# Error rows by a PE transpose of the predictions, cell 1's h in one operation, and a reordered phase in a two-group recurrent kernel

## What is computed

```python
encoded   = tanh(xt @ We + st @ Ue + be)                       # 24 values
new_state = tanh(xt·Wx + st·Ws + bk)                           # 8 candidates of 32
mem = concat([[encoded, err]], mem[:-1])                       # 20 entries of 25
a        = relu(mem.reshape(b, -1) @ enc_w1 + enc_b1)          # 64
agent_in = relu(a @ enc_w2 + enc_b2)                           # 16
h1, c1 = lstm(agent_in, h1, c1);  h2, c2 = lstm(h1, h2, c2)    # 16 each
gate  = softmax(h2 @ gate_w + gate_b)                          # 8
theta = clamp01(mean(|mem[:, :10, -1]|) * 2.5)
gate  = gate * theta + gate_before * (1 - theta)
st    = sum_c gate[c] * new_state[c];  pred = clamp01(st[-1]);  err = pred - yt
```

## Time and profile before

| | |
|---|---|
| median of 3 runs | 5459.47 us |
| profiled execution | 5460.57 us |
| its span, first to last instruction | 5458.7 us |
| span over 512 items | 10.66 us |
| PE matmul busy | 5391.8 us (99%) |
| VectorE, ScalarE, GpSimd busy | 4479.8, 3807.2, 2421.7 us (82, 70, 44%) |
| granted TensorE clock, mean | 0.998 |

### The profile page before, as it was taken

How to read it: one execution, slowest core, us unless ns; L and a number is a source line. 1 busy time by engine, 2 the same in 40 slices (tenths; PEclk the granted TensorE clock), 3 DMA queues, 4 the chain that set the end, 5 groups by cost and what they waited for, 6 DMA issues and landing times.

```text
span 5458.7 us, 188210 instructions
## 1 busy us (share of the span) xinstructions
PE 5391.8 (99%) x67584; PEld 3426.0 (63%) x67584; DVE 4479.8 (82%) x12336; ACT 3807.2 (70%) x9729; POOL 2421.7 (44%) x4613
## 2 busy tenths in 40 slices
PE   8999999999999999999999999999999999999998
PEld 5666666666666666666666666666666666666665
DVE  7888888888888888888888888888888888888887
ACT  5777777777767777777777777777777777777775
POOL 3444444444444444444444444444444444444444
PEclk9999999999999999999999999999999999999999
DMA  2111111111111111111111111111111111111111
GB/s 69 29 29 32 29 32 29 32 29 32 29 32 29 32 29 30 31 29 32 29 32 29 32 29 32 29 32 29 30 31 29 32 29 32 29 32 29 32 29 40
DMA packets 299285, 172.38 MB, mean 32 GB/s; under 512 B 156734, under 2 KB 263882, under 8 KB 298714
## 3 DMA queue, kind: packets, MB, share of 16 engines
q1 hardware_dynamic: 293568, 159.42, 11.2%
q10 hardware_dynamic: 5146, 3.66, 0.2%
HBM read 74.65 MB, written 2.10 MB: 14 GB/s over the span
## 4 chain that ended last, share of the span: by engine, by line
PE 95%; DVE 4%; issue 1%; DMA 0%; POOL 0%; ACT 0%; DVEq 0%; ACTq 0%; POOLq 0%
PE a_ps L366 26%; PE chain L417 17%; PE cand_ps L338 9%; PE a_ps L377 9%; PE cand_ps L347 7%; PE chain L310 5%; PE chain L317 4%; PE chain L403 4%; PE chain L293 4%; PE a_ps L388 3%; PE chain L435 3%; PE cand_ps L330 3%; DVE mixed L799 1%; DVE state L817 1%; DVE added L720 1%
## 5 line engine op out<-in xcount | busy, mean ns | idle before, releaser
L366 PE MATMUL a_ps<-hist,w_hist 125*64 125x512 f16 x12288 | 1896.3, 383 | 24.1 <-DMA w_hist<-enc_table 24.1
L817 DVE TENSOR_REDUCE state<-mixed 128x64 f32<-128x512 f32 x2048 | 1353.4, 682 | 34.2 <-POOL mixed L920 0.8
L920 POOL TENSOR_TENSOR mixed<-cand,gate 128x512 f32<-128x512 f32 x1024 | 1281.1, 1272 | 48.6 <-POOL gate L908 12.5
L554 ACT ACTIVATE cand<-cand_ps 128x512 f32<-128x512 f32 x2048 | 1101.8, 593 | 91.1 <-PE cand_ps L347 90.6
L417 PE MATMUL chain<-cell_in,cell_w 128*64 128x128 f32 x16384 | 1120.7, 278 | 19.8 <-DVE cell_in L735 19.8
L886 POOL TENSOR_TENSOR one_theta<-ones,theta 128x8 f32<-128x8 f32 x512 | 103.4, 202 | 2241.0 <-DVE theta L702 2241.0
L417 PEld LDWEIGHTS chain<-cell_in,cell_w 128*64 128x64 f32 x16384 | 889.2, 136 | 271.5 <-DVE cell_in L735 211.8
L366 PEld LDWEIGHTS a_ps<-hist,w_hist 125*64 125x64 f16 x12288 | 681.4, 109 | 536.2 <-issue 141.7
L561 ACT ACTIVATE gates<-chain 128x384 f32<-128x384 f32 x1024 | 502.0, 490 | 726.3 <-PE chain L417 726.1
L735 DVE SCALAR_TENSOR_TENSOR cell_in<-gates,tanh_c 64x128 f32<-64x128 f32 x2048 | 582.5, 284 | 127.0 <-ACT tanh_c L571 113.4
L720 DVE SCALAR_TENSOR_TENSOR added<-gates 128x256 f32<-128x256 f32 x1024 | 537.1, 524 | 141.2 <-ACT gates L561 141.2
(11 more groups left out here) (76 smaller groups left out, 6823.8 us busy)
## 6 DMA issues: line engine op xcount, KB each, us to landing
x_sb<-in_x_l SPq DMA_DIRECT2D x260, 256.0 KB, 2.7
hist<-entry_parts SPq DMA_DIRECT2D x2048, 25.0 KB
w_hist<-enc_table SPq DMA_DIRECT2D x258, 128.0 KB, 2.4
y_rows<-in_y_l SPq DMA_DIRECT2D x260, 8.0 KB
ys<-in_y ACTq DMA_DIRECT2D x1, 2048.0 KB, 16.3
preds_out<-preds SPq DMA_DIRECT2D x1, 2048.0 KB, 7.5
cand<-in_encoder ACTq DMA_DIRECT2D x1, 640.0 KB, 3.8
cell_w<-in_cell ACTq DMA_DIRECT2D x2, 256.0 KB, 4.5
```

Of the source, the lines that this page charges most:

```text
L366: nc.tensor.matmul(a_ps[g][ENC * half:ENC * half + ENC, :], w_hist[0:HROWS, w_slot(u), kk, wp, :], hist[0:HROWS, xp, k, at:at + 512], star ...
L554: ins = nc.scalar.activation(cand[:, g, q // 2, :, q % 2, :, :].rearrange("p h s c -> p h (s c)"), cand_ps[q][:, :].rearrange("p (h k) -> ...
L817: V.tensor_reduce(state[:, g, hf, 2 * pair:2 * pair + 2, :], mixed[:, pair, hf, :, :, :], AX, ALU.add)\
L920: G.tensor_tensor(mixed[:, 0, :, q, :, :], cand[:, g, 0, :, q, :, :], over_s, ALU.mult)\
```

## The change

Error rows:

- `pred_now` is laid out `(h q)` instead of `(a h l)`, and VectorE computes it (`prediction(old)`) right after the mix sums.
- PE transposes it (`prediction_transpose`, two is_transpose matmuls with a stationary operand of 4 columns, moving `ident`) into partitions 0 to 3 of `cand_ps[0]`, between `history(cur, 2, 1, 3)` and `encoded_s`.
- `errors` subtracts y from those rows in PSUM, and now stands ahead of cell 1's h. `at_least_zero` and `clamped` are gone. y lies in partitions 0 to 3.
- `w_ue` has 96 columns and `w_we` 128; the products that use them go in blocks of 32 columns: three for L317, four for L310 (before: 64 and 36).

Cell 1's h: one 128-partition operation into `h_second`; the gate logits use it in two matmuls of 64 moving columns (before: four of 32). Two VectorE copies (`keep_hidden`, after `below_peak`) bring it to `cell_in[1]`.

Copy of h: GpSimd copies all of `cell_in[1]` of a group to `cell_in[0]` (`next_hidden`, after its mixes), and the waits for it move from PE's cell 0 to the two `agent_input` operations. ScalarE's two copies are gone.

Orders: ScalarE takes the third candidates' tanh after `encoder1`. On PE one history set moves from before `encoder2` to after it, and all of `history(new, 1)` now stands between `encoder2` and `candidates_bias`. VectorE's `thetas` follow cell 1's h.

```diff
-ENTRY_ROWS = (slice(0, HALF), slice(HALF, ER))
+ENTRY_ROWS = tuple(slice(S * r, S * r + S) for r in range(ZR // S))
+CHAIN_ROWS = tuple(slice(S * r, S * r + S) for r in range(P // S))
@@ PE
+            def prediction_transpose(item):
+                g, n, u = item
+                pe.wait_ge(q_pred, n)
+                pe.wait_ge(q_cand[0], n)
+                for hf in range(HF):
+                    last = nc.tensor.matmul(cand_ps[0][0:Q, P * hf:P * hf + P],
+                                            pred_now[:, g, Q * hf:Q * hf + Q], ident[:, :], is_transpose=True, start=True, stop=True,
+                                            skip_group_check=True)
+                last.then_inc(q_predps, 1)
@@ encoded_x
-                for rows in ENTRY_ROWS:
+                for rows in CHAIN_ROWS:
@@ cell_gates
-                    pe.wait_ge(q_hnext, n)
                 else:
+                    pe.wait_ge(q_hkept, n)
@@ gate_logits
-                for hf in range(HF):
-                    for rows in CELL0_OUT:
-                        last = nc.tensor.matmul(chain[g][rows, 0:TILES * C]
-                                                .rearrange("p (a h k) -> p a h k", a=2, h=HF)[:, :, hf, :],
-                                                cell_in[1][:, g, hf, rows], gate_w[:, hf, :],
-                                                start=False, stop=True, skip_group_check=True)
+                for rows in CELL0_OUT:
+                    last = nc.tensor.matmul(chain[g][rows, 0:TILES * C], h_second[:, g, rows], gate_w[:, :],
+                                            start=False, stop=True, skip_group_check=True)
@@ PE phase
                     history(cur, 2, 1, 3)
-                    history(cur, 3, 0, 1)
+                    prediction_transpose(cur)
                     encoded_s(cur)
                 if new:
                     history_waits(new, extra)
                     history(new, 0, 0, 1)
                 if cur:
-                    history(cur, 3, 1, 2)
+                    history(cur, 3, 0, 1)
                 if old:
                     logit_bias(old)
-                if new:
-                    history(new, 0, 1, 2)
-                if old:
                     gate_logits(old)
                 if cur:
-                    history(cur, 3, 2, 3)
+                    history(cur, 3, 1, 3)
                     encoder1_now(cur)
                     bias_of_cell(cur, 0)
                 if new:
-                    history(new, 0, 2, 3)
-                    history(new, 1, 0, 2)
+                    history(new, 0, 1, 3)
                 if cur:
                     encoder2(cur)
+                if new:
+                    history(new, 1)
+                if cur:
                     candidates_bias(cur)
-                if new:
-                    history(new, 1, 2, 3)
@@ ScalarE phase
-                    at_least_zero(new)
                     encoded(new)
                     entry_high(new)
                 if cur:
-                    candidates(cur, 2)
                     exponentials(cur)
                 if new:
                     encoder1(new)
                 if cur:
-                    next_hidden(cur, 0)
+                    candidates(cur, 2)
@@ VectorE
-                dve.wait_ge(q_rl, n)
-                V.scalar_tensor_tensor(entry[ZR:ER, g, :], clamped[ZR:ER, g, :], 1.0,
-                                       y_rows[ZR:ER, x_slot(u), g, :], ALU.min, ALU.subtract)\
+                dve.wait_ge(q_predps, n)
+                V.tensor_tensor(entry[ZR:ER, g, :], cand_ps[0][0:Q, 0:COLS], y_rows[0:Q, x_slot(u), g, :],
+                                ALU.subtract)\
+            def second_hidden(item):
+                g, n, u = item
+                dve.wait_ge(q_tanhc[1], n)
+                dve.wait_ge(q_out_gate[1], n)
+                V.scalar_tensor_tensor(h_second[:, g, :], gates[1][:, g, 0, :], 1.0, tanh_c[1][:, g, :],
+                                       ALU.add, ALU.mult).then_inc(q_h[1], 1)
+            def keep_hidden(item):
+                g, n, u = item
+                dve.wait_ge(q_h[1], n)
+                for hf in range(HF):
+                    rows = CELL1_OUT[hf]
+                    last = V.tensor_copy(cell_in[1][rows, g, hf, :], h_second[rows, g, :])
+                last.then_inc(q_hkept, 1)
@@ VectorE phase
                     mix_sum(old, 1, 1)
+                    prediction(old)
...
                     cell_value(cur, 1)
-                    thetas(cur)
-                if old:
-                    prediction(old)
-                if cur:
-                    new_hidden(cur, 1, 0)
-                    new_hidden(cur, 1, 1)
                 if new:
                     errors(new)
                 if cur:
+                    second_hidden(cur)
+                    thetas(cur)
                     peaks(cur)
                     below_peak(cur)
+                    keep_hidden(cur)
@@ GpSimd
+            def next_hidden(item):
+                pool.wait_ge(q_hkept, n + GROUPS)
+                G.tensor_copy(cell_in[0][:, g, :, :], cell_in[1][:, g, :, :]).then_inc(q_hnext, 1)
                     mix_quarter(old, 0)
+                    next_hidden(old)
```

More of the change, by code:

```diff
@@ L572, in value_tanh @@
                     .then_inc(q_tanhc[c], 1)
-            def next_hidden(item, hf):
-                g, n, u = item
-                rows = CELL0_OUT[hf]
-                if hf == 0:
-                    act.wait_ge(q_h[0], n)
-                last = nc.scalar.activation(cell_in[0][rows, g, hf, :], cell_in[1][rows, g, hf, :], ACT.Copy)
-                if hf == HF - 1:
-                    last.then_inc(q_hnext, 1)
             def exponentials(item):
@@ L612, in phase @@
                     cell_tanhs(new, 0)
-                if cur:
-                    next_hidden(cur, 1)
-                if new:
                     cell_tanh_out(new, 0)
@@ L677, in _ @@
                 link(V.tensor_scalar(some, some, scale, None, ALU.mult))
-            link(V.tensor_scalar(gate_w[:, :, :], gate_w[:, :, :], 0.5, None, ALU.mult))
+            link(V.tensor_scalar(gate_w[:, :], gate_w[:, :], 0.5, None, ALU.mult))
             dve.wait_ge(s_hist0, 1)
@@ L683, in _ @@
             dve.wait_ge(s_y[0], 16)
-            first = y_rows[ZR:ER, 0, :, :].rearrange("p g b -> p (g b)")
+            first = y_rows[0:Q, 0, :, :].rearrange("p g b -> p (g b)")
             link(V.tensor_scalar(first, first, -1.0, None, ALU.mult))
@@ L727, in cell_value, with first_hidden @@
                                        added[c][:, g, 0, :], ALU.mult, ALU.add).then_inc(q_cell[c], 1)
-            def new_hidden(item, c, hf):
+            def first_hidden(item, hf):
                 g, n, u = item
-                rows = (CELL0_OUT, CELL1_OUT)[c][hf]
-                if hf == FIRST_HALF[c]:
-                    dve.wait_ge(q_tanhc[c], n)
-                    dve.wait_ge(q_out_gate[c], n)
-                last = V.scalar_tensor_tensor(cell_in[1][rows, g, hf, :], gates[c][rows, g, 0, :], 1.0,
-                                              tanh_c[c][rows, g, :], ALU.add, ALU.mult)
-                if hf != FIRST_HALF[c]:
-                    last.then_inc(q_h[c], 1)
+                rows = CELL0_OUT[hf]
+                if hf == 0:
+                    dve.wait_ge(q_tanhc[0], n)
+                    dve.wait_ge(q_out_gate[0], n)
+                last = V.scalar_tensor_tensor(cell_in[1][rows, g, hf, :], gates[0][rows, g, 0, :], 1.0,
+                                              tanh_c[0][rows, g, :], ALU.add, ALU.mult)
+                if hf == HF - 1:
+                    last.then_inc(q_h[0], 1)
+            def second_hidden(item):
[11 more added lines that the diff above has]
+                last.then_inc(q_hkept, 1)
             def agent_input(item, hf):
@@ L953, in keep_prediction @@
                 step, ring = place(item, extra)
[L954 to L956 removed]
+                pool.wait_ge(q_pred, n + GROUPS)
+                pred = pred_now[:, g, :].rearrange("p (h a l) -> p a h l", h=HF, a=2)
+                G.tensor_copy(by_quarter(preds[:, tiles, bass.ds(step, 1)]), pred).then_inc(q_predout, 1)
             def turn_start(turn):
@@ L991, in zeros @@
         return np.zeros(shape, np.float32)
-    out = dict(we=zeros(P, ER), ue=zeros(P, ER), wx=zeros(P, NS), ws=zeros(P, NS), bk=zeros(P, HF, NS),
-               encoder=zeros(P, MEM, ENC), now=zeros(P, 2, P), enc2=zeros(P, 2 * H), gate_w=zeros(P, HF, Q, C),
+    out = dict(we=zeros(P, P), ue=zeros(P, ZR), wx=zeros(P, NS), ws=zeros(P, NS), bk=zeros(P, HF, NS),
+               encoder=zeros(P, MEM, ENC), now=zeros(P, 2, P), enc2=zeros(P, 2 * H), gate_w=zeros(P, 2, HF, 2, C),
                cell0=zeros(P, HF, 4, HALF), cell1=zeros(P, HF, 4, HALF))
@@ L1005, in weights_laid_out @@
         out["ue"][rows, q:ZR:Q] = of("Ue")
-        out["ue"][S * q + S - 1, ZR + q] = 1.0
         out["wx"][rows] = of("Wx").transpose(1, 2, 0).reshape(D_IN, NS)
```

(2 more changed lines are left out.)

57 lines of the change are left out of this document (27 added, 30 removed).

## The result

The changed kernel takes 5989.6 us (median of 4 runs, 5987.1 to 5994.6) against 5458.9 us (4 runs, 5458.0 to 5461.2) on the same chip: ratio 1.0973, 95% interval 1.0954 to 1.0992. The direction was forecast, the size was not: 5735 us with a range to 5840. Of the +531 us, about 320 lie in the phases and about 210 at the loop's edge, of which the prediction had nothing.

The account below looks back on a forecast made before the run. PE's work from phase to phase bounds the kernel. Terms +0.10, +0.49, +0.12 and -0.13 sum to +0.58 us, taken as +0.56; 512 phases give 287, less 9 at the edge: 5738, stated as 5735 us, range 5540 to 5840.

Parts of the forecast that it names:

- Once a turn VectorE is late at the loop's edge ... 51 x 0.17 = 9 us: At the loop's edge PE idles 0.39 us a turn with VectorE late; slack covers about 0.17, gaining 9 us.
- The phase: PE's work from phase to phase: sum +0.58 us, taken as +0.56, times 512 is 287 us.
- the 0.13 of waits that were to go: On PE, 0.08 us of waiting goes before cell 1's gates and 0.05 before the next phase's state transposes.
- Changes of shape: On PE, four new changes between 64-wide and 32-wide tiles, 0.12 us each (bounds 0 and 0.15): +0.48 a phase.
- Rival A: Tile widths of 32 and 64 mix freely, so all four changes are free: 5548 us; chance 0.14.
- Transposes: Two fp32 prediction transposes of 128 moving columns added on PE, one after the other: 0.24 us (0.22 to 0.39).
- rival B: Transposes take the whole array, so one more change of shape before the encoded rows: +0.09 a phase, 5781 us; chance 0.14.
- the sign that was named for B: Weight loads idle with no releaser ("issue") ahead of the encoded rows from the state, right behind the transposes.
- The moved set: Second encoder layer starts 1.88 us after the first whatever stands between; the moved history set costs its 0.22 later.
- Gate logits, error path: Four logit matmuls for eight: 0.14 us, -0.12; errors and one h end at 2.19, so logits start at 2.25.
- Off the path: VectorE's two copies (0.16 to 0.29 each) and GpSimd's copy (0.19 to 0.67) fall in idle time, costing nothing.
- Rival C: Waits on the loop through VectorE and ScalarE, not PE's work, set the phase: faster, 5374 us; chance 0.08.

Follow-up runs that it names:

- after_head96: Changed kernel with PE's loop head at slot 96 of the 256-instruction fetch block instead of slot 0: 5779.4 us, 1.0581.
- after_no_pred: Changed kernel, one history set back ahead of the second layer, no prediction transposes in the loop: 5610.9 us; the pair's second, state rows 64 wide: 5609.4 us.
- after_set_back: Changed kernel, loop head at slot 96, with one history set moved back ahead of the second encoder layer: 5663.0 us, 1.0368.
- before_one_h: Kernel before with only the hidden state's part: cell 1's h in one operation, two logit matmuls, VectorE's and GpSimd's copies: 5573.3 us, 1.0209.
- before_exp_first: Kernel before with the exponentials put ahead of the third candidates' tanh on ScalarE, nothing else: 5428.0 us, 0.9940.
- before_pad_2853: Kernel before with twenty satisfied waits a phase added to PE, giving 2853 instructions a turn as in the changed kernel: 5619.8 us, 1.0294.
- after_head8: Changed kernel with PE's loop head at slot 8 instead of slot 0: 5874.6 us, 1.0758.
- after_head24: Changed kernel with PE's loop head at slot 24 instead of slot 0: 5829.5 us, 1.0673.

## Why the prediction was wrong

**The step that failed** is "Once a turn VectorE is late at the loop's edge ... 51 x 0.17 = 9 us". The edge was priced as a wait for VectorE, with a gain. That wait did go: 19.8 us in all before, 0.6 in after_head96, whose edges are 11 us cheaper than before's. But in its place PE's own instruction stream stands there: 2.8 us of idle time, then the half clock, 4.6 us a turn. That is 210 us by after_head96 and most of the 255 us that were missing. The change adds ten PE instructions a phase; their price as instructions was counted, their place in the fetches was not, and it stood in the sum at nothing. What makes the fetch late in this stream is open.

**The phase**, +0.56 forecast, +0.62 measured; with it and a cheap edge, after_head96 is 44 us above 5735, inside the range. The total is closer than its parts: +0.12 up to the first layer (forecast +0.10), -0.06 from there to the second (0), +0.51 from there to cell 0 (+0.49), +0.05 behind it (-0.01, since of the 0.13 of waits that were to go little went). Point by point:

- *Changes of shape*, four at 0.12: right, places and price, but there is a fifth. Rival A falls. The rule of the Trainium skill that a change of tiling mode drains the engine (TensorEngine Tiling (Array Packing), Key Properties) holds here for 32 and 64 wide: 0.10 us between starts in the after_no_pred pair.
- *Transposes*, 0.24: 0.31 measured, and rival B was right here. The 0.24 called itself the streaming price, while the prediction's own row gives 0.11 for 128 fp32 columns. In the trace the second transpose starts 0.11 behind the first, and L328 0.20 behind the second: 0.09 more than streaming, the size of the other changes, with 0.22 us of idle weight loads ahead of L328, the sign that was named for B. As history to transposes also shows 0.10, their shape is neither the 64-wide nor the 32-wide one. That it is the whole array isn't shown, and no run has them in another form.
- *The moved set*: right. L388 to L399 1.82 (forecast 1.88), and the set cost 0.25 us behind it, by after_set_back (forecast 0.22).
- *Gate logits, error path*: right; 0.14 us, and L445 at 2.28.
- *Off the path*: right for the changed kernel, but barely, and for a reason that hides: PE's changes of shape and the set make its own work longer than the chain through VectorE and GpSimd. In after_head96 cell 1's gates start 0.150 us behind h of cell 0, and 0.146 is what the kernels show that wait for it. In the kernel before, the hidden state's edits cost 114 us (before_one_h), where by the prediction's prices they gain. The bounds for the copies (0.16 to 0.29) came from operations that don't lie beside GpSimd's: the two take 0.84 us there and 0.91 in the changed kernel. The cover would have failed at once, had PE's part been cheaper, as after_no_pred shows.
- *Rival C* said that a loop through VectorE and ScalarE sets the phase. For the kernel before this is half true: in every phase cell 1's gates start 0.055 us behind VectorE's h of cell 0, so PE waits for it, and what moves it is when the mixes end, which goes by VectorE's queue and the exponentials' start (before_exp_first, -32 us without touching PE). The changes of shape are real all the same. The prediction priced that wait at 0.08 and ruled the rival out from PE's rows alone.

The time was missed by an unpriced term, not by the range of a priced one.

## What to carry to other kernels

Before adding instructions to the engine that bounds a hardware loop, look in the trace at how long its closing branch lasts and when the last instruction fetch ahead of it starts; the same work can gain or lose 3.6% by where the loop begins. An operation "in idle time" of VectorE or GpSimd is free only if nothing of the other engine that shares its port lies under it: follow the end of the long GpSimd operation. And where several parts of a change meet, try each alone in the kernel before, since one part's cost can hide another's.

## What was not expected of the hardware

- PE's closing branch lasts 0.3 to 0.5 us where the last instruction fetch starts 2.2 us or more ahead of it, and otherwise ends 2.3 to 2.9 us behind that fetch's start: up to 3.9 us. In the long case the granted clock then shows 0.61 over 3.4 us (1.2 GHz for most of it). Two streams with the same count and tail (after, before_pad_2853) differ, 3.0 to 3.9 against 0.4 to 0.8 us.
- The price varies from turn to turn in one execution (after_head8, after_head24).
- Two fp32 transposes with 4 stationary columns cost a change of shape on either side, 0.10 and 0.09 us, beside 64-wide and 32-wide matmuls.
- A satisfied wait that pushes a late one into an instruction of its own costs 0.06 us on ScalarE or VectorE and 0.09 on PE, 40 us in all here.
